# ScalarE lays out a sub-block's sums in two halves in two slots, and copies edge features in the eighth slot of a super block

## The reference

```python
def _egat_layer(nf, ef, src, dst, W_ni, W_nj, W_fij, W_node, attn, bias):
    f_out = (nf @ W_ni)[src] + (nf @ W_nj)[dst] + ef @ W_fij + bias
    f_out = leaky_relu(f_out, 0.2).reshape(-1, H, D)          # H = 4, D = 32
    e = einsum('ehd,hd->eh', f_out, attn)
    emax = segment_max(e, dst); a = exp(e - emax[dst])
    a = a / segment_sum(a, dst)[dst]
    h = (nf @ W_node).reshape(-1, H, D)
    return segment_sum(h[src] * a[:, :, None], dst), f_out
for l in range(3):
    nfh, efh = _egat_layer(...)
    nf, ef = nfh.mean(axis=1), efh.mean(axis=1)
x = x + nf
```

## Time and profile before

| | us |
|---|---|
| median of three runs | 2903.08 |
| lowest and highest of them | 2897.58, 2905.69 |
| the profiled execution | 2908.63 |
| its span, from the first to the last instruction | 2906.8 |
| busy in it: DVE | 2435.2 (84%) |
| PE | 2274.3 (78%) |
| POOL | 2060.1 (71%) |
| PEld | 1753.4 (60%) |
| ACT | 1503.3 (52%) |

### The profile page before, as it was taken

The page is one execution under the profiler, slowest core; times in us unless marked ns, Lnnn a source line. Parts: engine busy times, 40 slices in busy tenths (PEclk is TensorE's granted clock), DMA queues, the critical chain, the costliest instruction groups (busy, mean ns, idle before and its releaser), DMA issues.

```text
span 2906.8 us, 49919 instructions
## 1 busy us (share of the span) xinstructions
PE 2274.3 (78%) x15871; PEld 1753.4 (60%) x16027; DVE 2435.2 (84%) x5972; ACT 1503.3 (52%) x3713; POOL 2060.1 (71%) x2167
## 2 busy tenths in 40 slices
PE   3388888888888468888888887836888888888884
PEld 1266666666665356666666665535767666666653
DVE  7299999999997458999999998736898899898874
ACT  0056565656565225656565655613555555555552
POOL 6777777777772577777777777567777777777753
PEclk9699999999998689899999999958898898898885
DMA  7235454545442324444444443333334343343322
GB/s 256 69 97 160 116 158 119 161 116 159 118 132 93 106 68 143 118 139 140 138 134 140 142 138 103 106 112 96 103 103 124 115 128 106 114 127 102 103 89 80
DMA packets 139273, 353.90 MB, mean 122 GB/s; under 512 B 43895, under 2 KB 96027, under 8 KB 120207
## 3 DMA queue, kind: packets, MB, share of 16 engines
q1 hardware_dynamic: 67216, 296.09, 28.7%
q0 software_dynamic: 68960, 39.71, 9.3%
q10 hardware_dynamic: 2838, 14.91, 1.3%
HBM read 137.79 MB, written 212.77 MB: 121 GB/s over the span
## 4 chain that ended last, share of the span: by engine, by line
DVE 40%; PE 20%; issue 14%; ACT 12%; POOL 9%; DMA 3%; SPq 1%; DVEq 0%; ACTq 0%; POOLq 0%
DVE U L1383 17%; POOL rows L561 7%; DVE rows L1304 6%; PE f_ps L702 6%; DVE lr L1315 5%; PE f_ps L711 5%; DVE U L1368 4%; PE pick_ps L671 4%; ACT up L928 3%; ACT xT L848 3%; ACT f_low L857 3%; PE xT_ps L692 2%; DVE z L1394 2%; DVE rows L1405 2%; PE f_ps L721 2%
## 5 line engine op out<-in xcount | busy, mean ns | idle before, releaser
L561 POOL DMA_INDIRECT rows<-nf_tab,src_sb x1995 | 1890.8, 948 | 638.0 <-issue 588.0
L711 PEld LDWEIGHTS f_ps<-w_out,lr 128*128 128x128 f32 x4836 | 658.8, 201 | 357.7 <-issue 201.2
L1383 DVE TENSOR_TENSOR_SCAN U<-wide_ps,U 128x272 f32<-128x272 f32 (+2 forms) x1272 | 801.3, 692 | 3.3 <-ACT wide_ps L916 2.4
L702 PE MATMUL f_ps<-xT,w_edge 97*128 97x512 f32 x1212 | 697.7, 659 | 39.1 <-ACT ef_new L879 26.3
L671 PE MATMUL pick_ps<-nf_part,z 125*128 125x160 bf16 x6345 | 565.2, 247 | 208.4 <-issue 166.5
L671 PEld LDWEIGHTS pick_ps<-nf_part,z 125*128 125x128 bf16 x6345 | 507.8, 104 | 236.7 <-issue 189.7
L711 PE MATMUL f_ps<-w_out,lr 128*128 128x36 f32 (+1 forms) x4836 | 627.4, 269 | 27.2 <-DVE lr L1315 24.7
L1315 DVE TENSOR_TENSOR lr<-f_ps,f_low 128x512 f32<-128x512 f32 x606 | 407.5, 672 | 203.6 <-ACT f_low L857 202.9
L857 ACT ACTIVATE f_low<-f_ps 128x512 f32<-128x512 f32 x606 | 361.6, 597 | 325.6 <-PE f_ps L702 325.5
L692 PE MATMUL xT_ps<-ident,rows 128*97 128x128 f32 x2418 | 416.1, 297 | 92.1 <-issue 37.0
L916 ACT ACTIVATE wide_ps<-e_dw 128x289 f32<-128x289 f32 (+2 forms) x636 | 245.3, 402 | 348.7 <-DVE U L1383 343.0
(11 more groups left out here) (162 smaller groups left out, 1148.5 us busy)
## 6 DMA issues: line engine op xcount, KB each, us to landing
u_tab<-up SPq DMA_DIRECT2D x144, 1088.0 KB, 4.5
s_nd<-edge_first SPq DMA_DIRECT2D x48, 768.0 KB
rows<-nf_tab,src_sb POOLq DMA_INDIRECT x1995, 2.4
ef_tab<-ef_new SPq DMA_DIRECT2D x32, 768.0 KB
ef_st<-ef_tab SPq DMA_DIRECT2D x32, 768.0 KB
z<-fifth_tab SPq DMA_DIRECT2D x141, 96.0 KB
edge_first<-s_nd ACTq DMA_DIRECT2D x16, 768.0 KB
ef_st<-in_edge_attr_dram SPq DMA_DIRECT2D x16, 672.0 KB
```

Of the source, the lines that this page charges most:

```text
L561: eng.indirect_dma_start(rows[q % RING][:, c * K:c * K + D], None, nf_tab[:, :], bass.IndirectOffsetOnAxis(ap=src_sb[:, t:t + 1], axis=0)) ...
L702: eng.matmul(f_ps[n % 2][:, 0:grp_w(g) * P], w_edge[l][:, :], xT[y][0:K, 0:grp_w(g) * P], start=True, stop=True).then_inc(f_ready, 1)
L711: mm = eng.matmul(f_ps[n % 2][:, u * m:(u + 1) * m], lr[y][:, u * P:(u + 1) * P], w_out[l][:, 0:m], start=True, stop=True)
L1383: last = eng.tensor_tensor_scan(uh[:, c0 * w:c1 * w], dbc[h % 2][:, 0:(c1 - c0) * w], uh[:, c0 * w:c1 * w], 0.0, ALU.mult, ALU.add)
```

## The change

`lay_out` is split in two functions: `lay_half(k, half)` copies the sums of one half of the sub-block's columns, `lay_max(k)` the maxima. In the steady loop the first half follows `carry` in the place `i` = 1, as the whole did, the second half and the maxima come a slot later, ahead of `take_picks`. `put_ef` moves from the third to the eighth slot of the super block. In the tail `lay_out` calls all three in a row; the one sub-block of which the loop leaves the second half over gets it just behind the loop. `up_ready` now rises by three for each sub-block, and who waits for it counts so (the diff also has VectorE's two waits).

```diff
 def store_u(k):
-    eng.wait_ge(up_ready, 2 * k + 2)
+    eng.wait_ge(up_ready, 3 * k + 3)
...
-def lay_out(k):
+def lay_half(k, half):
     s = k % 2
-    if k >= 2:
-        eng.wait_ge(u_out[s], 16 * (k // 2))
-    eng.wait_ge(sums_done, 4 * k + 4)
+    if half == 0:
+        if k >= 2:
+            eng.wait_ge(u_out[s], 16 * (k // 2))
+        eng.wait_ge(sums_done, 4 * k + 4)
     w = sub_w(k % NB)
-    eng.activation(up3[s][:, 0:w, 0:CH].rearrange("p t (c h) -> p t c h", h=H),
-                   carry_of(U[s], w)[:, :, 1:w + 1, :]
+    t0, t1 = half * (w // 2), (half + 1) * (w // 2)
+    eng.activation(up3[s][:, t0:t1, 0:CH]
+                   .rearrange("p t (c h) -> p t c h", h=H),
+                   carry_of(U[s], w)[:, :, 1 + t0:1 + t1, :]
                    .rearrange("p c t h -> p t c h"),
                    ACT.Copy).then_inc(up_ready, 1)
+def lay_max(k):
+    s, w = k % 2, sub_w(k % NB)
     eng.activation(up3[s][:, 0:w, CH:UR],
...
+def lay_out(k):
+    lay_half(k, 0)
+    lay_half(k, 1)
+    lay_max(k)
...
 if i == 1 and g >= 2 * GB:
     carry(k)
-    lay_out(k - 1)
+    lay_half(k - 1, 0)
+if i == 2 and g >= 2 * GB:
+    lay_half(k - 1, 1)
+    lay_max(k - 1)
 if g >= 0 and i == PICK - 1 and g // GB + 2 < NPICK:
     take_picks(g // GB + 2)
-if g >= 0 and g % GS == 2 and g // GS + 1 < NS:
+if g >= 0 and g % GS == 7 and g // GS + 1 < NS:
     put_ef(g // GS + 1)
...
 k = kl + (END - 1) // GB
+lay_half(k - 1, 1)
+lay_max(k - 1)
 widen(k, 2)
```

More of the change, by code:

```diff
@@ L1326, in soften @@
                         if k >= 2:
-                            eng.wait_ge(up_ready, 2 * k - 2)
+                            eng.wait_ge(up_ready, 3 * k - 3)
                             eng.wait_ge(dbc_ready, 4 * (k - 1))
```

## The result

| | before | after |
|---|---|---|
| median, us | 2906.11 (20 runs) | 2922.41 (20 runs) |
| lowest and highest, us | 2895.28, 2914.70 | 2902.49, 2935.21 |
| span of the profiled execution, us | 2906.8 | 2929.1 |
| mean granted TensorE clock in it | 0.892 | 0.853 |
| first to last `leaky`: first, second, third layer, us | 820.6, 832.0, 866.5 | 821.3, 836.6, 883.0 |

The ratio is 1.0051, 95% interval 1.0033 to 1.0070. The lengths by layer are differences of starts of `leaky` rows (two for each layer). The two layers in which I had forecast most of the gain show none of it: the first is 0.7 us longer, the third 16.5.

The account below looks back on a forecast made before the run. VectorE was taken as the bound, waiting in slot 11 of C for ScalarE's `f_low`, held behind the layout. The terms -7.8 - 1.0 - 4.9 + 1.1 + 4.5 = -8.1 us gave 2895.0 us, range 2881 to 2911.

Parts of the forecast that it names:

- the first move: Half the layout and the maxima leave ScalarE's slot 10, so VectorE's wait of 0.52 us in slot 11 goes to nothing.
- C: Third sub-block of a super block, slots 9 to 12; VectorE waits in slots 10, 11 and 12; to shorten by 0.52 us.
- the first term: First layer: the wait in slot 11 saved in 15 super blocks, 15 x 0.52 = 7.8 us.
- The clock's term: TensorE's longer pause before the pick at the end of B lowers its clock in 2 of 15 first-layer super blocks: +4.5 us.
- Rival 4: Slower by the clock: first-layer pause at the end of B, 2.27 us per super block, ten falls, 2913.2 us; chance 0.15.
- B: Second sub-block, slots 5 to 8; VectorE never waits; the pause before the pick at its end grows from 1.13 to 2.0 us.
- A: First sub-block of a super block, slots 1 to 4; VectorE is the bound there and never waits.
- The third has it already: Third layer, granted clock already 0.88: no cost of further clock falls was counted there.
- The features in slot 8: `put_ef`, 1.57 us, moved to slot 8, delays `f_low` of slot 9 by at most 0.4 us, 1.9 free: cost 0.
- The second half in slot 11: Second half and maxima cost ScalarE 1.15 us in slot 11, covered by its wait of 1.65 for VectorE: taken as 0.
- rival 3: The wait only moves from slot 11 to the slot after: 0 to +1 us, 2903.5 us; chance 0.15.
- The price of two instructions for one: One more instruction per layout, paid in the 27 `lay_out` calls after the loops: 27 x 0.04 = 1.1 us.

Follow-up runs that it names:

- e6: The changed kernel with TensorE's fill burst held until the second half of the layout is done, and eight matmuls long, not four: 2867.34 us, ratio to before 0.9854.
- e5: The kernel before with a fill burst of eight matmuls, not four, the layout whole: 2875.38 us, ratio to before 0.9893.
- e7: e3 with fewer gathers in the second layer, 27 in a super block, not 39: 2848.23 us, ratio to before 0.9793.
- e11: The kernel of e6 measured once more, beside e12 on one chip: 2866.76 us, ratio to before 0.9862.
- e9: e6 with `put_ef` in the third slot again: 2874.46 us, ratio to before 0.9896.
- e12: The kernel of e9 measured once more, beside e11 on one chip: 2871.59 us, ratio to before 0.9870.
- e2: The kernel before with only `put_ef` moved to the eighth slot, the layout whole: 2905.49 us, ratio to before 0.9983.
- e3: The changed kernel with TensorE's fill burst of four held until the second half of the layout is done: 2874.16 us, ratio to before 0.9871.

## Why the prediction was wrong

I had forecast 2895 us, faster by 8.1; it came out some 16 us slower by the medians (2922.41 - 2906.11), above the range. Point by point:

**The bound and the first move were right.** Slot 11 lost its wait where the clock held, and the slots around it kept theirs. C gained 0.60 a super block, not 0.52. To measure the terms free of the clock, e6 is set against e5, which have nearly the same clock in all layers: first layer 808.9 - 815.7 = -6.8 (forecast -7.8), second 832.6 - 831.0 = +1.6 (-1.0, and bound by the gathers as e7 shows), third 836.6 - 840.3 = -3.7 (-4.9). The sum is -8.9, against -13.7. But whole layers are a rough measure: two profiles of one kernel differ by 1.7, 1.5 and 0.5 (e6 and e11), and by up to 12.7 in the third layer (e9 and e12), nearly all of it in the head and tail. Within the 15 super blocks e6 and e11 agree to 0.2 in the first and the third layer. There e6 stands below e5 by 721.8 - 713.2 = 8.6 in the first layer, and by 737.2 - 734.9 = 2.3 in the third. So the first term was right, and the third layer's came to about half. (e6 also holds the burst; in e5 `take_scores`, late as in before, does that.)

**The clock's term failed.** Taking the forecast terms as paid, the clock cost 0.7 + 7.8 = 8.5 us in the first layer, 4.6 + 1.0 = 5.6 in the second, 16.5 + 4.9 = 21.4 in the third: 35.5, where I had taken 4.5. Within the 15 super blocks alone it is 5.9 + 7.8 = 13.7, 3.9 + 1.0 = 4.9 and 13.8 + 4.9 = 18.7. (These are the two profiled executions; the medians lie 16.3 apart, not 22.3, so the typical cost is some 6 less.) Three steps of that term were wrong.
- *How many super blocks.* I took 2 of 15 in the first layer. Eight paid, for 1.6 or 2.1 each, where I had a price of 2.27. Rival 4 decided from six on, and so it did.
- *Where.* I looked at the end of B alone, and saw its pause grow to 2.0; it grew to 1.49, since the burst came 0.34 earlier and not 0.85: the pick did stay with VectorE's rows, as I said, but my estimate for the burst was too large. The end of A, which I did not price, had the longest pause before (1.81 in the median), and a growth of only 0.3 took it from 2 falls to 13. That VectorE "never waits" in A and B was also not so: `leaky` in slot 6, in B, stood still 0.99 and 0.96 us in two super blocks of the first layer of before, behind falls at the end of A, and 10.1 us in all in the third. The place nearest to the edge was the one to look at, not the one that moves most.
- *"The third has it already."* This was the dearest step: 21.4 us. A layer at 0.88 has still 0.88 to lose. At the end of A it had 10 falls and went to 12, but at the end of B it went from 5 to 14. That a part of it is low already bounds nothing.

The cover that I named for the second layer's clock, the gathers, did not hold wholly: 4.6 us came through.

**The rule that I weighed.** I put it against a row of the trace, took the row's side, and still chose a price near to the rule's zero. The Trainium skill, "TensorE: Matmul & The Clock Gate", section "Why this matters for your kernels", asks only that long pauses between bursts of matmuls be kept out. Read as if shorter ones cost nothing, it does not agree with the trace: here falls came in or right behind pauses of 2.11 and even 1.21 us. Another section of that page, "A second HAM failure mode: psum-queue depth-cycling", tells of another kernel in which frequent short idle spells between groups of matmuls make the clock swing between its levels. Such a swing is what these runs show, and e3 and e6 show what shorter spells give back. It would have spoken for rival 4.

**The rest.** The features in slot 8 cost nothing (e2). The second half in slot 11 found its cover: 0.90 us of wait were left of the 1.65. The wait in slot 12 kept its 0.39, so rival 3, by which the wait only moves, did not come. The price of two instructions for one was near: a half took 1086 ns in the mean of 288, where I had 1073. One statement was false: that every waiter counts three for a layout. TensorE's wait at the end of a layer (L779) still counts two for each, and so is passed early; the row behind it waits for VectorE's `jwT` in both kernels (0.78 us at 971.46 in after, six us behind the last layout), and it moved no time.

**What stays open.** In the third layer of after the pause at the end of B is shorter than before (1.21 against 1.52) and is followed by a fall more often (14 against 5). Six of these falls came 51.2 us apart, at the same place in their super blocks. So the last pause alone does not decide; what the engine did in the slots before it, which ran at the low clock after the fall at the end of A, may, but no run here separates the two.

## What to carry to other kernels

When an engine is let go earlier, look at every engine that waited for it: work that it used to hold back, such as a burst that keeps a clock up, goes early too, and the gap that this leaves may cost more than the wait that was saved. Price such a gap at the place that was nearest to the edge before, and in the stage that already suffers most. A filler belongs in the middle of the gap that it fills, and holding it back by a wait on purpose can pay: against the change that one wait was worth 1.8%, and with a longer burst 2.0%; against before it is 1.3 and 1.5%.

## What the runs showed of the hardware

- TensorE's granted clock fell in or right behind single pauses of 1.2 to 2.1 us. With the burst of 0.8 us moved from the start of the idle stretch (0.26 ahead of it, 2.11 behind) towards its middle (1.15 and 1.68, e3), 13 falls at one place became 2, though the pauses add up to more.
- A fall at the end of A that lasted over two picks cost 2.1 us in a sub-block of 16.3 us; many falls in the first layer were over at the next pick and cost nothing. The number of falls is no measure of the cost, the time at 1.2 GHz is nearer to it.
- Eight matmuls in the place of four, twelve more in a super block whose results nobody uses, made before itself 1.1% faster (e5).
